# VectorE's exponentials of an attention kernel: six chained passes over 512 columns in place of twelve interleaved ones over 256

## What is computed

```python
qh = _split_heads(q @ Wq + bq)        # 16 heads, depth 8
kh = _split_heads(k @ Wk + bk)
vh = _split_heads(v @ Wv + bv)
logits = jnp.einsum('bhsd,bhtd->bhst', qh, kh) / jnp.sqrt(DEPTH)
attn = jax.nn.softmax(logits, axis=-1)
out = jnp.einsum('bhst,bhtd->bhsd', attn, vh)
return out.transpose(0, 2, 1, 3).reshape(b, -1, D) @ Wo + bo
```

## Time and profile before

| | |
|---|---|
| median of 3 runs | 779.36 us (779.12 to 779.69) |
| the profiled execution | 778.57 us, of it span 776.9 us |
| busy: ScalarE, TensorE, VectorE, GpSimd | 93%, 90%, 85%, 25% of the span |
| first and last start of L810 in the trace | 73.9 and 737.6 us |
| granted TensorE clock | 0.999 of full speed over the span |

### The profile page before, as it was taken

How to read it: one execution, slowest core, us unless ns; L and a number is a source line. 1 busy time by engine, 2 the same in 40 slices (tenths; PEclk the granted TensorE clock), 3 DMA queues, 4 the chain that set the end, 5 groups by cost and what they waited for, 6 DMA issues and landing times.

```text
span 776.9 us, 36898 instructions
## 1 busy us (share of the span) xinstructions
PE 698.2 (90%) x15177; PEld 316.1 (41%) x15181; DVE 658.2 (85%) x1900; ACT 724.5 (93%) x651; POOL 191.9 (25%) x337
## 2 busy tenths in 40 slices
PE   9998899999999999999998999999999999899984
PEld 5564344334443344334433444334434443344342
DVE  4668888898889988998899888988899889988777
ACT  3467999999999999999999999999999999999964
POOL 4437222222222222222221222222222222122200
PEclk9999999999999999999999999999999999999999
DMA  5364111111111111111111111111111111111000
GB/s 141 118 181 163 39 43 36 38 43 44 37 35 43 47 40 35 41 47 41 36 40 44 45 36 38 45 46 38 37 39 46 43 36 40 41 37 35 14 2 27
DMA packets 37047, 38.39 MB, mean 49 GB/s; under 512 B 8968, under 2 KB 35402, under 8 KB 36948
## 3 DMA queue, kind: packets, MB, share of 16 engines
q1 hardware_dynamic: 35840, 36.52, 16.4%
q10 hardware_dynamic: 1108, 0.53, 0.2%
HBM read 30.14 MB, written 6.42 MB: 47 GB/s over the span
## 4 chain that ended last, share of the span: by engine, by line
ACT 59%; issue 25%; PE 11%; DVE 4%; ACTq 1%; DVEq 0%
ACT probs L810 58%; PE ps L1469 2%; PE ps L1422 1%; PE ps L1430 1%; PE ps L1460 1%; PE ps L1605 1%; PE ps L1413 1%; PE ps L1575 1%; PE ps L1395 1%; ACTq L822 1%; DVE gmax L1268 0%; ACTq L808 0%; DVE probs L1332 0%; DVE stats L914 0%; DVE sig L1128 0%
## 5 line engine op out<-in xcount | busy, mean ns | idle before, releaser
L810 ACT ACTIVATE probs<-ps 128x1536 f32<-128x1536 f32 (+1 forms) x536 | 663.4, 1366 | 3.5 <-PE ps L1575 3.4
L1605 PE MATMUL ps<-probs,v_op 64*9 64x512 f32 (+1 forms) x8256 | 522.6, 496 | 0.0
L1575 PE MATMUL ps<-q_op,k_op 59*32 59x512 bf16 x6432 | 335.9, 379 | 60.7 <-ACT probs L810 53.9
L1575 PEld LDWEIGHTS ps<-q_op,k_op 59*32 59x32 bf16 x6432 | 104.3, 89 | 338.2 <-issue 250.2
L1605 PEld LDWEIGHTS ps<-probs,v_op 64*9 64x9 f32 x8256 | 170.6, 86 | 64.2 <-issue 7.0
L676 POOL TENSOR_SCALAR e_pow<-e_t 128x512 int32<-128x512 int16 x135 | 83.5, 619 | 373.9 <-DVE e_t L1150 373.9
L1150 DVE TENSOR_SCALAR e_t<-ps 128x256 f32<-128x256 f32 x270 | 101.9, 419 | 78.2 <-PE ps L1575 77.8
L1186 DVE SCALAR_TENSOR_TENSOR e_f<-e_f,e_pow 128x256 f32<-128x256 f32 x270 | 109.4, 444 | 0.0
L1174 DVE SCALAR_TENSOR_TENSOR e_f<-e_u,e_f 128x256 f32<-128x256 f32 x270 | 103.3, 426 | 0.2
L1191 DVE SCALAR_TENSOR_TENSOR probs<-e_u,e_f 128x256 f32<-128x256 f32 x270 | 101.6, 415 | 0.0
L1165 DVE SCALAR_TENSOR_TENSOR e_u<-e_f 128x256 f32<-128x256 f32 x270 | 101.5, 418 | 0.0
(11 more groups left out here) (202 smaller groups left out, 260.6 us busy)
## 6 DMA issues: line engine op xcount, KB each, us to landing
k_op<-k_parts_dram SPq DMA_DIRECT2D x544, 36.0 KB
k_parts_dram<-k_parts SPq DMA_DIRECT2D x17, 288.0 KB, 3.0
k_op<-k_parts_dram SPq DMA_DIRECT2D x272, 12.0 KB
ctx_nat<-in_ctx_dram SPq DMA_DIRECT2D x16, 192.0 KB, 2.7
q_op<-q_parts_dram SPq DMA_DIRECT2D x32, 48.0 KB
q_parts_dram<-q_parts SPq DMA_DIRECT2D x2, 384.0 KB, 3.4
x_nat<-in_x_dram SPq DMA_DIRECT2D x1, 512.0 KB, 3.9
o_t<-att_rows SPq DMA_DIRECT2D x28, 16.0 KB
```

The lines of the kernel that those rows point to most:

```text
L810: act.activation(probs[:, b % NP].rearrange("p u t -> p (u t)")[:, 0:columns], ps[:, bank:bank + BU, :].rearrange("p u t -> p (u t)")[:, 0 ...
L1575: return pe.matmul(ps[a:a + P // G, bank, :], k_op[W2 * r:W2 * r + KR, kslot, i, P * j + a:P * j + a + P // G], q_op[W2 * r:W2 * r + KR, q ...
L1605: last = pe.matmul(ps[32 * k:32 * k + DH + 1, ACC[h], a:b], v_op[W2 * h:W2 * h + W2, slot, j, (DH + 1) * k:(DH + 1) * (k + 1)], probs[W2 * ...
```

## The change

Each of the six steps becomes one instruction over all 512 columns. It waits for the instruction directly before it. The counts change with it: `E_STEPS` from 10 to 5, `E_TAKEN` from 4 to 2, GpSimd's `powers` waits for 1 instead of 2, and TensorE's waits for `e_probs` count one per unit instead of two. All arithmetic stays. `halves` stays in use at the end of the program.

```diff
-E_STEPS = 10
-E_TAKEN = 4
+E_STEPS = 5
+E_TAKEN = 2
...
-                pool.wait_ge(e_step, E_STEPS * (e_count(ph, c) - 1) + 2)
+                pool.wait_ge(e_step, E_STEPS * (e_count(ph, c) - 1) + 1)
...
             halves = (slice(0, EH), slice(EH, EW))
+            whole = (slice(0, EW),)
...
-                for cols in halves:
+                for cols in whole:
                     score = ps[:, bank, 512 - EW + cols.start:512 - EW + cols.stop]
                     dve.tensor_scalar(e_t[:, cols], score, E_MIN, ROUND + EXP2_OFF, ALU.max, ALU.add
                                       ).then_inc(e_step, 1)
-                for n, cols in enumerate(halves):
+                for cols in whole:
                     score = ps[:, bank, 512 - EW + cols.start:512 - EW + cols.stop]
 
-                    dve.wait_ge(e_step, done + n + 1)
+                    dve.wait_ge(e_step, done + 1)
...
-                for n, cols in enumerate(halves):
-                    dve.wait_ge(e_step, done + 2 + n + 1)
+                for cols in whole:
+                    dve.wait_ge(e_step, done + 2)
...
-                for n, cols in enumerate(halves):
-                    dve.wait_ge(e_step, done + 4 + n + 1)
+                for cols in whole:
+                    dve.wait_ge(e_step, done + 3)
...
-                for n, cols in enumerate(halves):
-                    dve.wait_ge(e_step, done + 6 + n + 1)
+                for cols in whole:
+                    dve.wait_ge(e_step, done + 4)
                     dve.wait_ge(e_pow_ready, e_count(ph, c))
...
-                for n, cols in enumerate(halves):
-                    dve.wait_ge(e_step, done + 8 + n + 1)
+                for cols in whole:
+                    dve.wait_ge(e_step, done + 5)
...
-                            pe.wait_ge(e_probs, 2 * e_count(ph, 0))
+                            pe.wait_ge(e_probs, e_count(ph, 0))
```

More of the change, by code:

```diff
@@ L1656, in chunk @@
                         if s == 2:
-                            pe.wait_ge(e_probs, 2 * e_count(ph - 1, NC - 1))
+                            pe.wait_ge(e_probs, e_count(ph - 1, NC - 1))
                         if s < CT:
@@ L1661, in chunk @@
                         if s == 2:
-                            pe.wait_ge(e_probs, 2 * e_count(ph, c - 1))
+                            pe.wait_ge(e_probs, e_count(ph, c - 1))
                         values(slot, f - BPC, (0, 2, 1)[s], False, count=2 if s == 1 else 1)
@@ L1674, in chunk @@
                     elif s == 3:
-                        wait(e_probs, at(2 * e_count(ph, c - 1), 2))
+                        wait(e_probs, at(e_count(ph, c - 1), 1))
                         values(slot, f - BPC, 1 if c - 1 in E_EARLY else 2, False)
```

## The result

| | before | changed |
|---|---|---|
| median of 20 runs | 779.36 us (778.29 to 780.12) | 780.65 us (780.05 to 785.18) |
| ratio of the times | | 1.0025, 95% interval 1.0018 to 1.0031 |
| profiled execution, its span | 778.57, 776.9 us | 780.31, 778.6 us |
| first and last start of L810 | 73.9 and 737.6 us | 74.0 and 739.7 us |

The change makes the kernel slower by 0.25%: 1.9 us by the ratio, 1.3 by the medians, 1.7 between the profiled executions, whose granted clocks are 0.999 and 0.998. It lies in the attention: the exponentials of L810 are spread over 2.0 us more, the rest has not grown.

A forecast was written before the change was run, and what follows sets the result against it. ScalarE's exponentials were taken as the bound, with VectorE a helper. Seven phase changes at 0.43 us plus 0.16 us for the last phase's chunk 14 gave +3.2 us, forecast 782.6 us, range 780.8 to 785.8.

The forecast's parts named there:

- ScalarE is the bound, VectorE has idle time to spare: Whole kernel: ScalarE's exponentials run back to back, VectorE spares about 0.6 us per unit; at most 0.6 us to gain.
- The pass: One 512-column VectorE instruction: 0.687 us, plus a 0.033 us gap behind its predecessor, a pitch of 0.720 us.
- The unit: VectorE's six passes from one take of scores to the next: 4.29 us against 4.09, +0.20 us.
- c = 14: Chunk 14, taken without idle time: starts 0.20 us late, 0.04 spare, so ScalarE is pushed by 0.16 us.
- c = 0: First chunk of the next phase, taken without idle time: starts 0.16 + 0.20 = 0.36 us late.
- The result in that unit: Chunk 0's unit, with two accumulator transposes inside: first pass to result takes 0.07 us longer.
- The values' wait: TensorE's values of chunk 1 wait for VectorE's result, 0.43 us late; all reaches ScalarE, 0.43 us per phase change.
- c = 4 hidden: Chunk 4, 0.06 us idle before it: starts about 0.15 us late, hidden by 0.39 us before TensorE's next scores.
- No gap: Rival on chained VectorE passes: each starts as its predecessor ends, unit 4.13 us, time 779.4 us, no change; 14%.
- The values' wait hidden: Rival at the phase change: TensorE's values slip without moving the scores, 1.6 us lost, 781.0 us; 10%.
- Longer passes compound: Rival: passes of 0.743 us, units 0.54 us longer, a phase change costs about 1.6 us, some 791 us; 8%.
- the step at c = 15: Chunk 15 in the longer-passes case: it no longer absorbs all of its unit's 0.54 us growth.

The follow-up runs named there:

- one_steady: Whole 512-column passes only in chunks 1 to 12, semaphore increments of one, against the kernel before with halves everywhere; 778.19 us, ratio 0.9990.
- one_edges: Whole 512-column passes only in chunks 0, 13 and 16, semaphore increments of one, against the kernel before; 781.80 us, ratio 1.0037.
- free512: The changed kernel with whole passes reading a constant tile, so none waits for the last (VectorE's exponentials left out); 777.44 us, ratio 0.9985 to before.
- the swap: The changed kernel with TensorE taking VectorE's row tile one block later in chunk 1, exchanged with row tile 2; 779.14 us, ratio 0.9999 to before.
- one_1316: Whole 512-column passes only in chunks 13 and 16, against the kernel before; 780.34 us in one run.
- one_zero: Whole 512-column passes only in chunk 0, against the kernel before; 779.69 us in one run.
- w_edges: Whole passes only in chunks 0, 13 and 16, each raising its semaphore by two, against the kernel before; 790.57 us, ratio 1.0156.
- chained256: The kernel before, halves of 256 columns, each pass made to wait for the one directly before it; 883.83 us, ratio 1.1348.
- w_steady: Whole passes only in chunks 1 to 12, each raising its semaphore by two, against the kernel before; 781.05 us, ratio 1.0027.

## Why the prediction was right or wrong

The sign and the mechanism were right: slower, by lateness at c = 14 and at the change of phase, with nothing lost in between (one_steady, one_edges). The size was too large. I gave +3.2 us and 782.6; it is +1.9 by the ratio and +1.3 by the medians. The measured median, 780.65, lies 0.15 us under the lower end of my range, 780.8; the ratio times 779.36 gives 781.3, inside it.

**ScalarE is the bound, VectorE has idle time to spare**: right. With a unit of 3.8 us, free512 gains 7 x 0.05 = 0.35 us by the distances, less than the 0.6 that I had set as the most. By the runs it gains 1.2 us (0.5 to 1.9); what lies beyond the distances isn't accounted for.

**The pass**: 0.687 us was 0.692; the gap of 0.033 was right, the pitch 0.725 for 0.720.

**The unit** is the term of the sum that was mis-sized first. I kept 0.09 us that the sum of the form before falls short by, "most of that one pair per unit that lasts 0.83 instead of 0.76". In the changed kernel no pass is lengthened: 5 x 0.725 + 0.692 - 0.083 = 4.234, and 4.24 is measured, with nothing to add. The unit grew by 0.15 instead of 0.20. It was a cost beside GpSimd's copy that doesn't carry over to the chained passes (last section), and I had its row before me without asking what it stood beside.

**c = 14**: push of ScalarE 0.16 forecast, 0.12 measured. **c = 0**: start 0.36 late forecast, 0.22 measured: from the take of c = 13 it is 17.72 us (391.99 to 409.71) instead of 17.50 (391.30 to 408.80). That is the unit's 0.15 and a push of 0.07, since of the 0.12 some 0.05 is given back at c = 16. My sum carried the push of 0.16 through to c = 0 in full, without a look at c = 16; this is the second term that was mis-sized. In the kernel before, the exponential there follows 0.99 us after the one before, where 0.94 is usual; what held it was not tried. **The result in that unit**: +0.07 forecast, +0.09 to 0.10 measured (5.69 against 5.60). **The values' wait**: right, and by the swap the larger part of the loss. The result comes 0.31 late instead of 0.43 (by the rows its last pass ends 23.41 us after the take of c = 13 instead of 23.10), and all of it reaches ScalarE's exponential, as I had said. 7 x 0.31 = 2.2, and L810's span grew by 2.0, since one of the seven distances of before is 83.03: an exponential of c = 3 comes 0.23 late, behind scores that take 0.84 us instead of 0.61. The same exponential of the same phase is 0.21 to 0.23 late in one_steady, one_edges, one_1316 and one_zero, and on time in the changed kernel, so it isn't chance; its cause isn't known.

**c = 4 hidden**: right; its take now starts without idle time, and the exponentials there keep their pitch.

**The rivals.** *No gap*: out, by the pitch of 0.725 and by free512. *The values' wait hidden*: out, by the new row of the waits and by the swap. *Longer passes compound*: didn't happen, but w_edges shows the mechanism: at 4.61 us from take to take a phase costs 1.58 us more, and I had worked out 1.6 for a unit of about that size. That the two agree so closely is in part luck, since c = 14 and c = 15 keep their halves in w_edges, and the step at c = 15 that I had in the sum isn't there.

## What to carry to other kernels

In a helper engine's work a longer unit costs only where another engine waits for its result or where units follow each other with less idle time than the unit grows by; list those places in the timeline. Here 96 of 135 units stood elsewhere, and their change was free. Before splitting or merging instructions that depend on each other, compare pitches, not durations: two interleaved halves hid a chain cost of 0.12 us per pass that one whole pass shows. An added wait costs as much even where the data don't need it (chained256). If a wait at one place decides, look for work that can go ahead of it in the queue: two tiles swapped took back all that the change cost.

## What the runs showed of the hardware

**GpSimd's copy and VectorE's passes take turns, and what a pass loses depends on how much of the copy is left when it starts.** In the kernel before, GpSimd's copy and VectorE's passes beside it (c = 5 of a phase):

```profile
441.83 0.52 POOL L669 COPY v_op<-v_all 128x108 f32<-128x108 f32 x1 [0.90 <-PE ps L1605]
...
441.46 0.76 DVE L1174 SCALAR_TENSOR_TENSOR e_f<-e_u,e_f 128x256 f32<-128x256 f32 x2
...
442.13 0.83 DVE L1186 SCALAR_TENSOR_TENSOR e_f<-e_f,e_pow 128x256 f32<-128x256 f32 x2
```

The pass that starts during the copy lasts 0.08 us longer. Of the 1620 passes, 118 are over 0.05 us longer than the usual one, and all 118 start during such a copy. In the changed kernel the same place is:

```profile
442.85 0.63 POOL L669 COPY v_op<-v_all 128x108 f32<-128x108 f32 x1 [0.97 <-PE ps L1606]
...
442.65 0.69 DVE L1175 SCALAR_TENSOR_TENSOR e_f<-e_u,e_f 128x512 f32<-128x512 f32 x1
...
443.38 0.69 DVE L1187 SCALAR_TENSOR_TENSOR e_f<-e_f,e_pow 128x512 f32<-128x512 f32 x1
```

The passes are 0.69 us as everywhere, none is lengthened, and the copy takes 0.63 us instead of 0.52. It isn't their length that spares them: chained256, with chained passes of 256 columns, has one lengthened pass of 1620, and free512, with unchained ones of 512, has 112 of 810. In w_steady, where a gap of 0.10 us lies between the passes, the copy can start in the gap:

```profile
443.23 0.28 POOL L669 COPY v_op<-v_all 128x108 f32<-128x108 f32 x1 [0.90 <-PE ps L1612]
...
443.32 0.73 DVE L1180 SCALAR_TENSOR_TENSOR e_f<-e_u,e_f 128x512 f32<-128x512 f32 x1
```

Two things hold in these five traces (before, changed, chained256, free512, w_steady), but for at most a dozen of the 136 copies of each. A copy that starts beside no pass takes 0.27 us, and one that starts during a pass ends 0.12 to 0.21 us after that pass's end (the median is 0.13 in each kernel). A pass that starts during a copy is longer by what is left of the copy at its start less some 0.14 us: with 0.22 us left it is 0.08 longer (118 passes of the kernel before), with 0.18 left 0.03 longer (64 of w_steady), with 0.10 left not at all (128 of the changed kernel, 110 of chained256). An unchained pass starts 0.08 us ahead of its predecessor's end and so meets 0.22 us of the copy, a chained one starts 0.03 behind it and meets 0.10. The exceptions are copies of up to 1.06 us that last until the unit's last pass has ended and lengthen none; what decides that isn't known.

The Trainium skill (GPSIMD Engine Reference, "1. Specifications") has GpSimd contend with VectorE instructions that have two SBUF inputs. The trace agrees: all 118 lengthened passes have two.

**An instruction that raises a semaphore by two** was followed, in w_steady and w_edges, by a separate semaphore instruction before the next pass, and the pitch of dependent passes rose from 0.725 to about 0.80 us; with increments of one (one_steady, one_edges) neither is there. On a chain of short instructions, count in ones.
